# Router logits taken from the attention's parts instead of from the normalised rows, in a fused cross-attention and top-2 expert kernel

## The reference

```python
x = x + attention(layernorm(x), ctx, ctx, mask)      # 16 heads of 16, 375 context rows, 16 batches of 112 rows
x = x + moe(layernorm(x))                            # 8 experts, top 2, 512 hidden
# attention: q, k, v projections with bias; softmax(q k / 4) v; then  out @ Wo.T + bo
# moe, on 1792 tokens of 256:
gate_logits = flat @ router_w                        # [1792, 8]
gate_probs = softmax(gate_logits)
topk_w, topk_idx = top_k(gate_probs, 2)
topk_w = topk_w / clip(topk_w.sum(-1), 1e-9)
h = silu(einsum('td,edf->etf', flat, w1)); y = einsum('etf,efd->etd', h, w2)
out = einsum('etd,te->td', y, cw)                    # cw: the two weights, zero elsewhere
```

## Time and profile before

| what | value |
|---|---|
| median of 3 runs | 452.66 us (452.36 to 453.35) |
| the profiled execution | 451.87 us |
| its span from first to last instruction | 449.9 us |
| mean granted clock of TensorE | 0.959 of full speed |
| busy over the span | PE 411.5, VectorE 336.4, ScalarE 279.8, GpSimd 223.9 us |
| batch turns | about 55 to 251 us |
| last batch and routing, to the first expert matmul | 251 to 299.6 us |

### The profile page before, as it was taken

How to read it: one execution, slowest core, us unless ns; L and a number is a source line. 1 busy time by engine, 2 the same in 40 slices (tenths; PEclk the granted TensorE clock), 3 DMA queues, 4 the chain that set the end, 5 groups by cost and what they waited for, 6 DMA issues and landing times.

```text
span 449.9 us, 10827 instructions
## 1 busy us (share of the span) xinstructions
PE 411.5 (91%) x4219; PEld 382.5 (85%) x4219; DVE 336.4 (75%) x700; ACT 279.8 (62%) x381; POOL 223.9 (50%) x257
## 2 busy tenths in 40 slices
PE   7878999999999999999999996899999999999910
PEld 6747898999989999999998985789999999999910
DVE  7866778778877888787788778856886667776536
ACT  4767476665566665766555554648778777778600
POOL 6757443312444223433202764675787878876420
PEclk9999999999999999999999997589999999999975
DMA  7995676768866778766450259822222322332169
GB/s 213 237 199 155 135 158 131 150 150 162 197 159 156 153 140 189 157 132 128 96 120 3 75 205 365 272 68 73 85 80 85 95 83 94 83 82 73 47 231 306
DMA packets 44675, 64.32 MB, mean 143 GB/s; under 512 B 6801, under 2 KB 33570, under 8 KB 44626
## 3 DMA queue, kind: packets, MB, share of 16 engines
q1 hardware_dynamic: 38322, 50.40, 45.6%
q0 software_dynamic: 4096, 11.13, 8.2%
q10 hardware_dynamic: 2208, 2.12, 1.4%
HBM read 30.13 MB, written 9.28 MB: 88 GB/s over the span
## 4 chain that ended last, share of the span: by engine, by line
PE 79%; DVE 9%; DMA 5%; ACT 3%; issue 2%; POOL 1%; ACTq 0%; SPq 0%; DVEq 0%
PE ps L1546 41%; PE ps L1609 12%; PE ps L1626 9%; PE ps L1640 9%; PE ps L1915 2%; DVE x L1536 2%; PE ps L1653 2%; DMA q_stack<-attn_t_lo 1%; DMA y_back<-y_rows 1%; DVE neg_max L1105 1%; DMA keep<-keep_scratch 1%; PE ps L1709 1%; DMA keep_scratch<-keep_all 1%; PE ps L1665 1%; PE ps L1719 1%
## 5 line engine op out<-in xcount | busy, mean ns | idle before, releaser
L1105 DVE TENSOR_REDUCE neg_max<-ps 112x1 f32<-112x376 f32 x256 | 133.6, 545 | 41.4 <-PE ps L1609 36.5
L834 ACT ACTIVATE probs<-ps 125x1344 f32<-125x1344 f32 x64 | 82.8, 1294 | 43.4 <-PE ps L1626 38.2
L1609 PE MATMUL ps<-k_stack,q_stack 98*112 98x376 f32 x256 | 86.2, 369 | 3.7 <-DVE neg_max L1105 2.2
L604 POOL TENSOR_TENSOR k_lo<-k_f,k_hi 128x752 fp32r<-128x752 f32 x16 | 28.9, 1806 | 112.3 <-ACT k_hi L808 111.8
L765 POOL DMA_INDIRECT rows<-xn_rows,token_of_row x42 | 55.8, 1328 | 17.5 <-issue 12.5
L773 POOL DMA_INDIRECT y_rows<-y_out,slot_of_row x42 | 45.6, 1087 | 25.3 <-ACT y_out L1027 14.4
L1609 PEld LDWEIGHTS ps<-k_stack,q_stack 98*112 98x112 f32 x256 | 44.1, 174 | 16.3 <-DVE neg_max L1105 10.9
L1626 PE MATMUL ps<-q_stack,k_stack 100*125 100x224 f32 x384 | 52.6, 273 | 0.0
L1626 PEld LDWEIGHTS ps<-q_stack,k_stack 100*125 100x125 f32 x384 | 50.4, 188 | 0.7 <-ACT probs L834 0.5
L1546 PE MATMUL ps<-w_hi,h_hi 128*128 128x256 f32 x168 | 48.8, 290 | 0.4 <-DVE h_lo L1452 0.4
L1546 PE MATMUL ps<-flat_t_hi,w_hi 128*128 128x256 f32 x168 | 47.5, 283 | 1.3 <-DVE flat_t_lo L1430 1.3
(11 more groups left out here) (213 smaller groups left out, 1017.6 us busy)
## 6 DMA issues: line engine op xcount, KB each, us to landing
k_stack<-k_hi SPq DMA_DIRECT2D x32, 376.0 KB, 5.0
w_all<-w SPq DMA_DIRECT2D x2, 4096.0 KB, 18.8
k_stack<-k_lo SPq DMA_DIRECT2D x16, 376.0 KB, 5.5
ctx_raw<-ctx_t SPq DMA_DIRECT2D x32, 187.5 KB, 3.9
q_stack<-attn_t_hi SPq DMA_DIRECT2D x64, 56.0 KB
y_back<-y_rows SPq DMA_DIRECT2D x14, 256.0 KB, 5.1
x_rows_sb<-x_rows SPq DMA_DIRECT2D x4, 448.0 KB, 4.6
x<-x_tiles SPq DMA_DIRECT2D x7, 256.0 KB, 2.9
```

Source lines behind the costliest of these rows:

```text
L604: pool.tensor_tensor(kl[:, :, :], kf[:, :, :], kh[:, :, :].bitcast(F32), ALU.subtract)\
L834: act.activation(pf[j % 2][:, :, :], ps[0:CT, BK_ST:BK_ST + KT, 0:4 * S], ACT.Exp).then_inc(pf_ready, 1)
L1105: dve.tensor_reduce(neg_max[:, head:head + 1], ps[0:S, BK_MAX + s % 2, 0:CP], AX.X, ALU.max, negate=True).then_inc(max_read, 1)
L1609: pe.matmul(ps[0:S, BK_MAX + a, 0:CP], qs[b.ring][0:R_MAX, a, q, :], ks[b.ring][0:R_MAX, q, :], start=True, stop=True).then_inc(smax_done, 1)
```

## The change

The logits are no longer taken from the normalised rows. With x2 = x + A Wo^T + bo (A the attention's output) and a router whose columns have had their means taken off, the row's mean falls out, and the logits of a normalised row are (A (Wo^T R) + (x + bo) R) times the row's reciprocal root. The order of the experts doesn't need that root; it is multiplied in only for the softmax, in `below_maximum`. So:

- `column_means` (turn 1) and `router_through_output` (turn 4) make, on PE, the router's column means and Wo^T R; GpSimd centres the router and forms the low part. Three new inputs come in: x transposed (`x_t`), Wo's rows and bo as columns.
- `x_t` is loaded 256 tokens at a time in seven turns; GpSimd's `add_bias_t` adds bo.
- `route(n)` is now for one tile: four fp32r matmuls with th and tl and two plain fp32 ones with x_t. Tiles 0 to 10 are done at the ends of turns 6 to 14, tiles 11 to 13 in the last batch. Sums lie in the free columns of the bank of `quad_outputs`; ScalarE copies four tiles' sums away at a time ahead of `out_copy`.
- `flat_transpose`, `flat_high`, `flat_low` and `read_logits` are gone, and with them a copy of the router's parts at the start.
- Twelve tiles are early instead of eight. GpSimd makes 13 early lanes and one late one instead of 11 and 3. VectorE makes six of the early places of the first choice.
- Normalised rows have three buffers instead of six; ScalarE's queue stores units 6 and 7.
- The orders of PE and VectorE in the last batch are new.

```diff
-XN_RINGS = 6
+XN_RINGS = 3
-BK_FLAT = (3, 5, 3, 5, 1, 2, 3, 5)
-BK_RANK, BK_LATE, BK_PLACED, BK_TOKEN = 4, 6, 7, 0
+BK_RANK, BK_LATE, BK_PLACED, BK_TOKEN = 3, 6, 5, 0
+SUMS = QUADS * S
+SUM_TILES = (512 - SUMS) // (2 * E)
+ROUTED_IN = {6: (0,), 7: (1,), 8: (2,), 9: (3,), 10: (4,), 11: (5,), 12: (6, 7), 13: (8, 9), 14: (10,)}
+LOGITS_COPIED = {9: 0, 12: 1, 14: 2}
-EARLY_NT = 8
-POOL_LANES = (11, 3)
+EARLY_NT = 12
+POOL_LANES = (13, 1)
+SCALAR_PLACES = 6
...
+            def load_x_t(u):
+                sp.dma_start(xt[u % RINGS][:, :, :], x_t[:, :, TG * u:TG * (u + 1)].rearrange("k p n -> p k n"))\
+                    .then_inc(xt_in[u % RINGS], 16)
+
             for b in range(B):
                 turn(Batch(0, b))
+                if b == 3:
+                    sp.wait_ge(vproj_done, 8)
+                    sp.dma_start(xt[2][:, :, :], wo_rows.rearrange("k p n -> p k n")).then_inc(xt_in[2], 16)
+                if b in (4, 5):
+                    load_x_t(b - 4)
+                if b == 6:
+                    sp.wait_ge(sums_done, 2)
+                    load_x_t(2)
+                if b in (8, 10, 12, 13):
+                    u = {8: 3, 10: 4, 12: 5, 13: 6}[b]
+                    sp.wait_ge(logits_done, 2 * (u - RINGS + 1))
+                    load_x_t(u)
...
-            for u in range(6, 8):
-                write_rows(u)
...
+            def add_bias_t(u):
+                slot = u % RINGS
+                pool.wait_ge(xt_in[slot], 16 * (u // RINGS + 1 + (slot == 2)))
+                for k in range(KD):
+                    last = pool.tensor_scalar(xt[slot][:, k, :], xt[slot][:, k, :], bo_c[:, k:k + 1], None, ALU.add)
+                last.then_inc(xt_ready, 1)
...
             roots(6)
             normalise_rows(5)
+            lanes(0)
             roots(7)
-            lanes(0)
             lanes(1)
...
+                if b in LOGITS_COPIED:
+                    part = LOGITS_COPIED[b]
+                    act.wait_ge(logits_done, SUM_TILES * (part + 1))
+                    act.copy(logit_parts[:, SUM_TILES * part:SUM_TILES * (part + 1), :],
+                             ps[:, BK_OUT, SUMS:512].rearrange("p (n e) -> p n e", n=SUM_TILES)).then_inc(logits_read, 1)
...
             out_copy(last)
-            flat_high(3)
-            flat_high(4)
             attn_high(last)
-            for u in range(5, len(UNITS)):
-                flat_high(u)
+
+            def write_late_rows(u):
+                act.wait_ge(late_xn_ready, u - 5)
+                store_rows(act, u)
...
+            write_late_rows(6)
             for k, c in enumerate((1, 0)):
-                places_in_block(k, c, slice(0, EARLY_NT))
+                places_in_block(k, c, slice(0, EARLY_NT if c else SCALAR_PLACES))
             places_in_block(TOP, 1, slice(EARLY_NT, NT))
+            write_late_rows(7)
...
             def below_maximum():
                 step(dve.tensor_reduce(c0[:, :], logits[:, :, :], AX.X, ALU.max))
-                dve.tensor_tensor(shifted[:, :, :], logits[:, :, :], wide2(c0), ALU.subtract).then_inc(shifted_ready, 1)
+                step(dve.tensor_tensor(t0[:, :, :], logits[:, :, :], wide2(c0), ALU.subtract))
+                dve.wait_ge(row_rstd_ready, len(UNITS))
+                dve.tensor_tensor(shifted[:, :, :], t0[:, :, :], wide2(row_rstd), ALU.mult).then_inc(shifted_ready, 1)
...
             last = Batch(0, B - 1)
             row_vars(2)
-            flat_low(0)
             residual(4)
             row_vars(3)
-            read_logits(0)
+            row_vars(4)
             normalise(last.after(-1))
+            sum_early()
             attn_low(last.after(-1))
...
+            find_two(early_tiles)
             residual(5)
...
+            residual(6)
+            normalise(last)
+            place_rows(0, early_tiles, BK_RANK)
             row_vars(5)
...
+            attn_low(last)
             row_vars(6)
...
             normalise_late(6)
...
+            count_early()
+            sum_late()
+            find_two(late_tiles)
+            places_on_vector(slice(SCALAR_PLACES, EARLY_NT), 0)
+            lanes(0)
             residual(7)
             row_vars(7)
...
             place_rows(1, late_tiles, BK_LATE)
             lanes(1)
-            late_places_in_block()
+            places_on_vector(late_tiles, 1)
+            normalise_late(7)
             count_blocks()
...
+            def column_means():
+
+                pe.wait_ge(router_ready, 1)
+                pe.wait_ge(rw_in, 32)
+                product(ps[:, BK_OUT, SUMS:SUMS + E], [(mean_of[:, :], rw_raw[:, k, :]) for k in range(KD)])\
+                    .then_inc(sums_done, 1)
+
+            def router_through_output():
+
+                pe.wait_ge(router_ready, 2)
+                pe.wait_ge(xt_in[2], 16)
+                for j in range(KD):
+                    last = product(ps[:, BK_OUT, SUMS + E * j:SUMS + E * (j + 1)],
+                                   [(xt[2][:, k, P * j:P * (j + 1)], rw_raw[:, k, :]) for k in range(KD)])
+                last.then_inc(sums_done, 1)
+
+            def route(n):
+
+                if n == 0:
+                    pe.wait_ge(router_ready, 3)
+                newest = (P * (n + 1) - 1) // S
+                pe.wait_ge(th_ready, KD * (newest + 1))
+                pe.wait_ge(tl_ready, KD * (newest + 1))
+                pe.wait_ge(xt_ready, n // 2 + 1)
+                m, half = slice(P * n, P * (n + 1)), slice(P * (n % 2), P * (n % 2 + 1))
+                at = SUMS + 2 * E * (n % SUM_TILES)
                 for k in range(KD):
...
+                    pe.matmul(ps[:, BK_OUT, at:at + 2 * E], th[:, k, m], rw[:, k, :], start=k == 0, stop=False)
+                    pe.matmul(ps[:, BK_OUT, at:at + E], tl[:, k, m], rw[:, k, 0:E], start=False, stop=False)
+                for k in range(KD):
+                    last = pe.matmul(ps[:, BK_OUT, at:at + E], xt[n // 2 % RINGS][:, k, half], rw_raw[:, k, :],
+                                     start=False, stop=k == KD - 1)
                 last.then_inc(logits_done, 1)
...
                 outputs(b, 1)
+                if b.n == 1:
+                    column_means()
+                if b.n == 4:
+                    router_through_output()
+                for n in ROUTED_IN.get(b.n, ()):
+                    route(n)
```

More of the change, by code:

```diff
@@ L250, in xattn_moe_kernel @@
         cursor["at"] = rows_at
-        xn2 = [sb(f"xn2_{p}", [P, 2, D]) for p in range(RINGS)]
+        xt = [sb(f"x_t{p}", [P, KD, TG]) for p in range(RINGS)]
         cursor["at"] = hidden_at
@@ L293, in xattn_moe_kernel @@
         assert cursor["at"] <= last_query_at, "the zeros lie where the queries' first low part was"
+        cursor["at"] = last_query_at
+        mean_of = sb("mean_of", [P, P])
+        router_mean = sb("router_mean", [P, E])
+        router_f = sb("router_f32", [P, KD, E])
+        logit_parts = sb("logit_parts", [P, EARLY_NT, 2 * E])
+        assert cursor["at"] <= last_query_at + 4 * KD * TG, "the router's sums lie where the first step's rows come"
+        cursor["at"] = last_query_at + 4 * KD * TG
+        xn2 = [sb(f"xn2_{p}", [P, 2, D]) for p in range(XN_RINGS)]
         cursor["at"] = last_query_at
@@ L1955, in _ @@
             quad_outputs(before, 2)
-            flat_transpose(0)
+            quad_scores(last, 0)
             project_output(4)
-            quad_scores(last, 0)
+            route(11)
             quad_outputs(before, 3)
-            flat_transpose(1)
-            route(0)
             quad_scores(last, 1)
@@ L1964, in _ @@
             quad_outputs(last, 0)
-            flat_transpose(2)
+            quad_scores(last, 2)
             attn_transpose(before)
-            quad_scores(last, 2)
             project_output(5)
@@ L2039 @@
         "w2": np.ascontiguousarray(np.asarray(L0_ffn_w2)).reshape(E, KF, P, D),
+        "x_t": halves(x.reshape(T, D).T),
+        "wo_rows": halves(L0_xattn_Wo),
+        "bo_cols": columns(np.asarray(L0_xattn_bo).reshape(1, D)),
     }
```

191 lines of the change are left out of this document (65 added, 126 removed).

## The result

The changed kernel takes 468.5 us in the median of 4 runs (466.71 to 470.22), the kernel before 452.55 beside it: a ratio of 1.035 with a 95% interval of 1.031 to 1.039. It is slower, as predicted, but by 16 us and not by 9, and 468.5 lies outside the range. The profiled execution took 466.71 us around a span of 465.0, so the traces differ by 465.0 - 449.9 = 15.1 us. One run of a later variant (the variances first, 471.66 us) was in a slower state and is left out of that variant's numbers.

A forecast was written before the change was run, and what follows sets the result against it. PE bounds the batch turns; in the routing stage a chain hops between engines until read_lanes. 11.9 - 2.6 = +9.3 us on 451.87 gives 461.2, with 0.8 for the median 462.0 us; range 456.5 to 467.0.

The forecast's parts named there:

- Part 1: Batch turns: routing and router products added on PE lengthen them by 11.9 us in all, up to the end of turn 13.
- The split: Turns with routing: cutting the block of 48 quad_outputs records in two costs 0.13 us plus 0.08 for the change-over.
- Part 2's gain: Last batch and routing: the new order of engines ends read_lanes at 288.75 instead of 291.34, a gain of 2.6 us.
- the step that failed: Behind read_lanes: list, plan, gather and first weights are not edited, so the end of read_lanes measures the routing stage.
- Rival (d): Last row stores: they land late beside w2 and hold the first gather; priced at +3, 465 us; chance 0.10.
- the signs of being wrong: Turns staying near 13.7 us, records stepping at 0.03 or 0.22, or the gather waiting for rows.
- 3.9 us of leeway: Last row store, about 286.7, to first gather, 290.6: landing time beyond 3.9 us costs one us for each us.
- 0.8 was allowed from the kernel before: Whole kernel: the median was put 0.8 us above the profiled execution, as in the kernel before.
- The four passes for true fp32: Added fp32 calls: each loads weights four times, 26 calls cost 5.8 us more, 467.8 us; chance 0.06.

The follow-up runs named there:

- e2: Changed kernel with the fp32 products on x_t left out of route, so other experts are chosen: 460.91 us, ratio to the kernel before 1.0196.
- e3: Changed kernel with the routing block of a turn ahead of the second share of its outputs: 465.89 us, ratio to the kernel before 1.0307.
- e7: Changed kernel with VectorE's variances of units 5 and 6 ahead of the last batch's normalise and the early places: 463.61 us.
- e4: Changed kernel with GpSimd's roots of the last unit after 8 of its 13 early lanes, not after all: 464.12 us.
- e5: Changed kernel with only the first two experts' w2 sent at first, the rest once the first rows are gathered: 469.60 us.
- e10: Changed kernel with the first tile of each two-tile turn routed mid-turn, behind values(1), the second at the end: 468.55 us.
- e14: Changed kernel with routing ahead of second outputs, project_output(4) before last scores, variances of units 5 and 6 first, last roots after 8 early lanes: 457.99 us.
- e9: Changed kernel with variances of units 5 and 6 first on VectorE and the last unit's roots after 8 of 13 early lanes: 462.71 us.
- e13: Changed kernel with routing ahead of second outputs, project_output(4) before the last batch's first scores, variances of units 5 and 6 first: 460.12 us.

## Why the prediction was wrong

From 462.0 to 468.5 are 6.5 us. By the forecast's own steps:

- **Part 1, right.** 12.3 for 11.9, 0.3 of the difference ahead of the added products; eight records 0.11 apart, two a narrow fp32 product (e2), turns of 14.86 for 14.84. The split was 0.31 for 0.21 (e3). +0.4.
- **Part 2's gain, mis-sized: 1.1 for 2.6.** The chain is the one laid out, with GpSimd idle 6.74 us ahead of unit 5's roots and `normalise_late(7)` waiting 2.63 for the last ones. On the old clock (12.34 less) it slips by steps: the max_rows landed in 2.78 and not 2.2 (scores 0.6 later); `row_vars(5)` ended 1.1 late; unit 5 was normalised 1.3 late; 13 lanes took 10.6, not 10.2; `read_lanes` ended at 290.2, not 288.75. The landing and the longer lanes make 1.0 of that; most of the rest is time between instructions, which I had left out when I laid durations end to end. e7 shows that GpSimd's start hung on VectorE's order. +1.5.
- **"What stands behind it (list, plan, gather, first weights) is not edited, so I measure that stage by this instant": the step that failed.** The stage behind `read_lanes` was edited, through what it reads: the last rows are normalised and stored behind 13 lanes. Rival (d) named it and priced it at +3, and a gather that waits for rows stood among the signs of being wrong, but it had 0.10 and was left out of the sum. Its 3.9 us of leeway also lacked the 0.8 us from a landing to the gather's start (305.49 to 306.31). The store took 5.13 us from 300.36, and the first gather came 3.74 us after `read_lanes` instead of 1.80: 1.94. That delay cost twice more: the second gather is issued in 1.95 instead of 0.96 beside VectorE's split of w1, and PE, idle 4.07 us, transposes the first rows in 1.12 instead of 0.66, at a granted clock of 0.50 (311 to 315) where it was 1.00 (297 to 299). +3.4 in all. e4 and e5 each brought this stage back to 8.3 us, the one with an earlier store, the other with a quicker one: shown.
- **The expert steps** are 0.5 longer, the time outside the span 0.3 shorter; the cause of both is open.
- **The median stands 1.8 above the profiled execution**, where 0.8 was allowed from the kernel before. +1.0. Part of it may be the falls of the clock told of below; that is not shown.

0.4 + 1.5 + 3.4 + 0.5 - 0.3 + 1.0 = 6.5.

The trace of the kernel before bears on the step that failed. Its last store of rows, begun at 285.54 on SyncE behind w2, took this long:

```profile
DMA to landing us min/median/max: 6.6/6.6/6.6
```

So the last rows landed at 292.1, and the list of tokens was ready at 292.26: the two paths ended within 0.2 us of each other. Counted from batch 13's `attn_high`, the change made the list 1.1 us earlier and the last rows 1.0 later, so none of the tail's gain could reach the gather.

The four passes for true fp32 that the Trainium skill counts ("FP8 and Floating Point Precision", section TensorE Precision Notes), weighed in the forecast at 467.8, would have come near the result for the wrong reason: the trace has two records a product, and leaving the two out took 0.44 off a turn, where four would have taken 0.89.

## What to carry to other kernels

When work is moved off one path, look again at the path that runs beside it: in the kernel before, the last rows and the list of tokens were ready within 0.2 us of each other, so what was won in the listing alone could not move the gather, and what was lost in the rows did. A small store that must land soon should neither be queued behind a large load nor run beside one; 128 KB took 1.7 us alone and 5.1 to 5.4 beside w2. And a chain laid out end to end from durations leaves out the time between them: here it came out 1.5 us short in 38.

## What the runs showed of the hardware

**The granted clock can fall while PE is never idle.** Stretches around the two tiles of turn 12, of the changed kernel's first profile, then of its second:

```profile
229.00:233.00 4.00, 4.00 (x70) 3.54 (x69) 1.24 (x6) 2.60 (x4) 2.07 (x7) 1.00 0.24 72
233.00:237.00 4.00, 4.00 (x50) 3.58 (x49) 3.02 (x7) 1.30 (x4) 2.68 (x3) 1.00 0.96 232
```

```profile
229.00:233.00 4.00, 4.00 (x71) 3.50 (x70) 1.52 (x5) 2.60 (x4) 1.66 (x7) 1.00 0.16 34
233.00:237.00 4.00, 4.00 (x37) 3.22 (x37) 1.72 (x4) 0.65 (x2) 3.08 (x3) 0.57 0.97 243
```

The same code, busy throughout, goes from 2.4 to 1.2 GHz for some 3 us in one execution and not in the other; the turn takes 18.2 instead of 16.73. It happened in 6 of the 16 paired turns profiled with the pair as the change has it, never in the 14 where the pair was shorter, in another place or apart (e2, e3, e10 to e14). Ahead of a fall stand 1.9 us of products 8 and 16 columns wide. That they cause it is not shown: e10 moved them apart and its runs spread as far.

**A gather's issue on GpSimd doubles beside a two-input operation of VectorE**: 1.95 and 1.89 us under the split of w1, 0.94 to 0.96 apart from it (e4, e5, e9, e14). The split is two operations of 1.22 us one behind the other, and a gather that begins under the first ends 0.82 to 0.84 us after the end of that first one (both profiles of the changed kernel, e4, e5, e7, e9, e13, e14): the changed kernel's first at 309.70 (the first operation ends at 308.86), and one of e4, which began 0.75 us into it and took 1.30, at 310.67 (309.84). The Trainium skill, "SBUF — State Buffer", section SBUF: two separate sides, says that the two engines share a pair of ports, which a VectorE operation with two SBUF inputs holds for the whole instruction against a GpSimd operation that reads SBUF. These rows agree, if the gather reads its row numbers there; that it is these ports is not shown by them.

**A queue can hold its engine.** SyncE stood 9.81 and 13.38 us in the issue of one 256 KB store while w2 filled its queue, against 0.4 us for most issues; in the kernel before it stood 15.04 us in a store of 128 KB, from 270.46 on, behind w2 as well.
